# A fused pre-norm linear-attention and FFN kernel: q rotated with channels on partitions, and three data movements handed to DMA

## The reference, cut to what matters

```python
h = layernorm(x)
q, k, v = h @ Wq.T, h @ Wk.T, h @ Wv.T          # each (32, 256, 8, 16)
g = h @ Wg.T
q = q * cos + rotate_half(q) * sin              # the same for k
kv, ksum, vsum = k^T v per head, k.sum(tokens), v.sum(tokens)
num = (q @ kv) * scale + vsum
den = (q . ksum) * scale + 256
o = num / den + conv5(v, lepe_w) + lepe_b       # depthwise conv, 5 taps along the tokens
x = x + (o * g) @ Wo.T
h2 = layernorm(x).astype(bfloat16)
y = (fp8(h2 / s_in) @ fp8(ffn_w / s_k)) * (s_in * s_k)
x = x + (y.astype(bfloat16) + ffn_b)            # written out
```

## Time and profile before

| | |
|---|---|
| Median of 3 runs | 174.56 us (174.33 to 174.72) |
| Profiled execution | 174.49 us, of which the span of the trace is 172.7 us |
| Mean granted PE clock | 0.985 of full speed |
| PE busy / PEld busy | 162.4 us (94%) / 137.7 us (80%) |
| DVE busy | 152.2 us (88%) |
| POOL busy | 137.4 us (80%) |
| ACT busy | 132.5 us (77%) |
| Chain that ended last | PE 85%, POOL 4%, DVE 3%, issue 3%, ACT 2% |

### The profile page before, as it was taken

How to read it: one execution, slowest core, us unless ns; L and a number is a source line. 1 busy time by engine, 2 the same in 40 slices (tenths; PEclk the granted TensorE clock), 3 DMA queues, 4 the chain that set the end, 5 groups by cost and what they waited for, 6 DMA issues and landing times.

```text
span 172.7 us, 3890 instructions
## 1 busy us (share of the span) xinstructions
PE 162.4 (94%) x1140; PEld 137.7 (80%) x1140; DVE 152.2 (88%) x281; ACT 132.5 (77%) x358; POOL 137.4 (80%) x163
## 2 busy tenths in 40 slices
PE   7999999999999999999999999999999999999730
PEld 2578988887879898998889898988998898978510
DVE  2298899989898999999899999989899899899944
ACT  3759757787987878896969888887787786667770
POOL 1468987777897888989898898996889875979871
PEclk9999999999999999999999999999999999999985
DMA  4930002004040404021030404040310220020224
GB/s 133 272 83 0 0 6 61 2 4 121 2 121 6 121 0 123 4 65 56 16 111 0 121 6 121 6 121 0 92 35 0 65 61 4 0 65 2 61 61 121
DMA packets 18966, 9.71 MB, mean 56 GB/s; under 512 B 1536, under 2 KB 18816, under 8 KB 18944
## 3 DMA queue, kind: packets, MB, share of 16 engines
q1 hardware_dynamic: 18368, 9.19, 18.6%
q10 hardware_dynamic: 576, 0.26, 0.6%
HBM read 5.25 MB, written 4.19 MB: 55 GB/s over the span
## 4 chain that ended last, share of the span: by engine, by line
PE 85%; POOL 4%; DVE 3%; issue 3%; ACT 2%; DVEq 0%; POOLq 0%; ACTq 0%
PE bank L1126 15%; PE bank L1210 9%; PE bank L1172 8%; PE p_num L1191 8%; PE bank L1137 8%; PE p_num L1183 8%; PE bank L1145 7%; PE bank L1161 4%; PE bank L1200 4%; PE bank L1116 4%; PE bank L1153 4%; PE bank L1083 3%; PE bank L1253 2%; PE bank L1219 2%; DVE yc L786 1%
## 5 line engine op out<-in xcount | busy, mean ns | idle before, releaser
L597 POOL TENSOR_TENSOR qk<-turned 128x512 f32<-128x512 f32 x32 | 40.3, 1274 | 3.1 <-DVE turned L826 2.9
L826 DVE TENSOR_TENSOR turned<-bank,turn 128x1024 f32<-128x1024 f32 x32 | 38.7, 1216 | 0.9 <-PE bank L1126 0.9
L841 DVE SCALAR_TENSOR_TENSOR acc<-bank,conv_w,acc 128x510 f32<-128x510 f32 (+1 forms) x48 | 34.8, 725 | 0.2
L1126 PE MATMUL bank<-w_qk,hT 128*128 128x256 f32 x128 | 32.8, 381 | 0.2
L370 ACT ACTIVATE h<-x,nmr,rs 128x128 bf16<-128x128 f32 x60 | 24.7, 485 | 3.9 <-POOL nmr L571 3.9
L306 ACT ACTIVATE h<-xs,nmr,rs 128x128 f32<-128x128 f32 x64 | 26.3, 484 | 0.6 <-POOL nmr L560 0.4
L557 POOL TENSOR_TENSOR rs<-ve,minus_half 128x4 f32<-128x4 f32 (+1 forms) x17 | 16.7, 980 | 12.5 <-ACT ve L297 12.5
L1126 PEld LDWEIGHTS bank<-w_qk,hT 128*128 128x128 f32 x128 | 22.6, 190 | 2.9 <-issue 0.3
L568 POOL TENSOR_TENSOR rs<-ve,minus_half 128x4 f32<-128x4 f32 (+1 forms) x17 | 16.6, 977 | 6.7 <-ACT ve L361 6.6
L609 POOL TENSOR_TENSOR acc<-acc,outer 128x508 f32<-128x508 f32 x16 | 20.3, 1271 | 1.0 <-DVE acc L841 1.0
L1137 PEld LDWEIGHTS bank<-w_v,hT 128*128 128x128 f32 x128 | 16.4, 191 | 4.7 <-issue 3.3
(11 more groups left out here) (88 smaller groups left out, 326.6 us busy)
## 6 DMA issues: line engine op xcount, KB each, us to landing
xs<-_attn_hidden_states_dram SPq DMA_DIRECT2D x15, 256.0 KB, 2.8
out_dram<-ob SPq DMA_DIRECT2D x15, 256.0 KB, 2.5
turn<-in_turn_dram SPq DMA_DIRECT2D x1, 512.0 KB, 4.7
xs<-_attn_hidden_states_dram SPq DMA_DIRECT2D x2, 128.0 KB, 2.8
out_dram<-ob SPq DMA_DIRECT2D x2, 128.0 KB, 2.1
mask<-in_mask_dram SPq DMA_DIRECT2D x1, 68.0 KB, 5.0
w_raw<-in_L_attn_Wq_dram ACTq DMA_DIRECT2D x1, 64.0 KB, 2.3
w_raw<-in_L_attn_Wk_dram ACTq DMA_DIRECT2D x1, 64.0 KB, 2.5
```

The lines of the kernel that those rows point to most:

```text
L597: nc.gpsimd.tensor_tensor(qk[:, u % 2, j].rearrange("p q t d -> p t q d"), turned[:, j, :, :, 0:D].rearrange("p a h (q d) -> p (a h) q d", ...
L826: nc.vector.tensor_tensor(turned[:, j], p_qk[j].rearrange("p a h d -> p a (h d)").unsqueeze(2).to_broadcast([P, TPB, 2, 2 * D]), turn[:], ...
L841: nc.vector.scalar_tensor_tensor(out=part, in0=p_vT[:, :, lo + off:hi + off], scalar=conv_w[:, k:k + 1], in1=part, op0=ALU.mult, op1=ALU.a ...
L1126: last = nc.tensor.matmul(p_qk[j][:, a].rearrange("p h d -> p (h d)"), hT[:, u % 3, t * P:(t + 1) * P], w_qk[:].rearrange("p a q d -> p (a ...
```

## The change

The diff has four parts, and with them all five lists of calls are written anew.

1. q is projected alone and with channels on partitions: the weight is the stationary operand and one matmul with 512 columns makes q^T of the unit. DVE multiplies it by cosine and signed sine (`turn_q_unit`). The swap of the channel halves goes across partitions, so two DMAs on SP's queue move 64 partitions each (`swap_q`), and POOL adds (`add_q`). `transpose_q` and `move_qT` are gone. k stays with tokens on partitions and is done for the whole unit at once (`project_k`, `turn_k_unit`, `add_k`).
2. h2 is turned by a transposing DMA on SP's queue (`turn_h2`) for units 0 to 13, and by PE as before for units 14 and 15. ACT quantises from SBUF.
3. The FFN product is one matmul with the weight stationary and 512 columns, so y has channels on partitions. ACT scales it (`move_y`) and in a second instruction adds the bias, which is now one number per partition (`add_bias`). A second transposing DMA turns it back (`turn_yc`), and POOL's `final_sum` reads that. POOL's `add_bias` is gone. The last unit stays as it was.
4. Convolution tap 0 leaves DVE: ACT writes its product to a buffer (`conv_outer(u, 1)`), POOL adds it in a second `sum_outer`.

The core of the diff:

```diff
+            def swap_q(u):
+                s = u % 2
+                sp.wait_ge(q_turned_done, count(u))
+                sp.dma_start(q_swapped[0:P // 2, s], q_turned[P // 2:P, s, 1]).then_inc(q_swapped_in[s], 16)
+                sp.dma_start(q_swapped[P // 2:P, s], q_turned[0:P // 2, s, 1]).then_inc(q_swapped_in[s], 16)
+            def turn_h2(u):
+                s = u % 2
+                sp.wait_ge(h2_done, count(u))
+                if u >= 2:
+                    sp.wait_ge(q8_done, count(u, 2))
+                sp.dma_start(h2T[:, s].rearrange("p (t k) -> p t k", t=TPU), h2[:, s].rearrange("p t d -> p (t d)"),
+                             transpose=True).then_inc(h2T_in[s], 16)
+            def turn_yc(u):
+                s = u % 2
+                sp.wait_ge(ycT_done, count(u))
+                if u >= 2:
+                    sp.wait_ge(ob_done, count(u, 2))
+                sp.dma_start(yc[:, s], ycT[:, s], transpose=True).then_inc(yc_in[s], 16)
...
-                    act.wait_ge(h2T_filled, count(u))
+                    if u < PE_H2:
+                        act.wait_ge(h2T_in[u % 2], h2T_count(u))
+                    else:
+                        act.wait_ge(h2T_filled, 1)
...
+                nc.scalar.activation(ybT[:, u % 2], p_y[:], ACT.Copy, scale=ysc[:, 0:1]).then_inc(yb_done, 1)
+            def add_bias(u):
...
+                nc.scalar.activation(ycT[:, u % 2], ybT[:, u % 2], ACT.Identity,
+                                     bias=fb_act[:, 0:1]).then_inc(ycT_done, 1)
...
+            def add_q(u):
+                s = u % 2
+                pool.wait_ge(q_swapped_in[s], 32 * (u // 2 + 1))
...
+                nc.gpsimd.tensor_tensor(qT[:, s], q_turned[:, s, 0], q_swapped[:, s], ALU.add).then_inc(qT_done, 1)
...
+            def turn_q_unit(u):
...
+                nc.vector.tensor_tensor(
+                    q_turned[:, s].rearrange("p c (j s) -> p c j s", j=BPU),
+                    p_q[:].rearrange("p (j s) -> p j s", j=BPU).unsqueeze(1).to_broadcast([P, 2, BPU, S]),
+                    turn_q[:].unsqueeze(2).to_broadcast([P, 2, BPU, S]), ALU.mult).then_inc(q_turned_done, 1)
...
+            def project_q(u, *freed):
...
+                nc.tensor.matmul(p_q[:], w_qk[:, 0].rearrange("p a d -> p (a d)"), hT[:, u % 3], start=True,
+                                 stop=True).then_inc(q_filled, 1)
...
-                    for t in range(TPU):
-                        last = nc.tensor.matmul(p_y[:, t * P:(t + 1) * P], q[:, t * P:(t + 1) * P], fwq[:],
-                                                start=True, stop=True)
-                    last.then_inc(y_filled, 1)
+                    nc.tensor.matmul(p_y[:], fwq[:], q, start=True, stop=True).then_inc(y_filled, 1)
...
-DVE_TAPS = (1, 3, 0)
-ACT_TAP = 4
+DVE_TAPS = (1, 3)
+ACT_TAPS = (4, 0)
```

More of the change, by code:

```diff
@@ L217, in build @@
         h2T_filled = sem("h2T_filled")
+        h2T_in = [sem(f"h2T_in{n}") for n in range(2)]
         q8_done = sem("q8_done")
@@ new lines, in _ @@
+            load_x(3)
+            swap_q(1)
+            load_x(4)
+            swap_q(2)
+            turn_h2(0)
+            load_x(5)
+            swap_q(3)
+            turn_yc(0)
+            turn_h2(1)
+            load_x(6)
+            swap_q(4)
+            turn_yc(1)
+            turn_h2(2)
+            load_x(7)
+            swap_q(5)
+            turn_h2(3)
+            store(0)
+            store(1)
+            turn_yc(2)
+            load_x(8)
+            swap_q(6)
+            turn_yc(3)
@@ L274, in _ @@
+            store(10)
+            turn_yc(12)
+            turn_yc(13)
+            store(12)
+            store(13)
+            turn_yc(14)
+            store_end(0)
+            store(14)
+            store_end(1)
             sp.wait_ge(ob_free[0], 16 + 16 * (U // 2))
@@ new lines, in _ @@
+            var_eps2(3)
+            move_hT(6)
+            quantise_if_small(2, is_small)
+            norm2(3)
+            move_v(6)
+            var_eps1(7)
+            move_y(2)
+            conv_outer(6, 0)
+            conv_outer(6, 1)
+            add_bias(2)
+            norm1(7)
+            quantise_if_small(3, is_small)
+            conv_middle(6)
+            var_eps2(4)
+            move_hT(7)
+            move_y(3)
+            add_bias(3)
+            for t in range(8, 10):
+                move_v(t - 1)
+                var_eps1(t)
@@ new lines, in _ @@
+            pow2(3)
+            final_sum(1)
+            add_q(5)
+            pow1(7)
+            sum_outer(5, 0)
+            add_k(6)
+            sum_outer(5, 1)
+            final_sum(2)
+            pow2(4)
+            add_q(6)
+            pow1(8)
+            sum_outer(6, 0)
+            add_k(7)
+            final_sum(3)
+            for t in range(9, 12):
+                sum_outer(t - 3, 1)
+                pow2(t - 4)
+                add_q(t - 2)
+                pow1(t)
+                sum_outer(t - 2, 0)
+                final_sum(t - 5)
+                add_k(t - 1)
@@ new lines, in _ @@
+            sum_outer(9, 1)
+            pow2(8)
+            pow1(12)
+            add_q(10)
+            sum_outer(10, 0)
+            final_sum(7)
+            sum_outer(10, 1)
+            add_k(11)
+            pow2(9)
+            add_q(11)
+            pow1(13)
+            sum_outer(11, 0)
+            add_q(12)
+            sum_outer(11, 1)
+            add_k(12)
+            final_sum(8)
+            pow1(14)
+            pow2(10)
+            sum_outer(12, 0)
+            add_k(13)
+            sum_outer(12, 1)
```

992 lines of the change are left out of this document (558 added, 434 removed).

## The result

The changed kernel takes 178.58 us (median of 4 runs, 177.85 to 180.07), the kernel before on the same chip 174.53 us. The ratio is 1.0243, 95% interval 1.0191 to 1.0294: 4.1 us slower. The forecast was 169.5 us, so its sign is wrong; the time lies inside the range of 163.5 to 181. The profiled execution took 180.07 us with a span of 178.3. Every time here is the median of all executions of its kernel; the ratios leave out four executions, each of another kernel, that ran in a slower state of the chip, and without them no median moves by more than 0.07 us.

The account below looks back on a forecast made before the run. PE's list was taken as the bound, DVE about 5% behind. Fourteen units saving 9.45 - 9.0 = 0.45 us give 6.3: 174.49 - 6.3 + 1.3 = 169.5 us; own range 163.5 to 173.9, 8-in-10 range 163.5 to 181.

Parts of the forecast that it names:

- The new waits: Waits on the added DMAs for h2, q's swap and y: hidden in the middle, with 2.8 us taken for a transposing DMA.
- the paragraph on SP's queue: SP's queue goes from two issues a unit to six, about 0.5 us each, so 3.1 of 9 us.
- Both cost nothing in the middle.: q's swap and y's turn back: POOL reads each one period later, so neither costs time in the middle.
- The turn of h2, 2.8 us under 3.35 of cover: ACT's quantisation waits for the turned h2; 3.35 us of other ACT work hides a 2.8 us DMA.
- Rival C: Slow transposing DMA stalls ACT's quantisation by the excess over 3.35 us per unit; 182.7 or 192 us in its cases; chance 0.18.
- PE's list, 8.72 us: PE's work per middle unit falls from 9.45 to 8.72 us, mainly by dropping the transposes of q and h2.
- rival D: The change does not do what it says: given no room, as FFN branches and turns are unconditional for these inputs.
- The 9.0 us that I allowed for waits among level engines: Period of a middle unit, 0.2 us above the largest engine sum; ends 8.8 and 9.3.
- DVE, ACT and POOL: Their work per middle unit after the change: DVE 8.25 us, ACT 8.81, POOL 8.57.
- The end, +1.3 us: Later last norm on ACT and unit 14's y going through a DMA add about 1.3 us; ends 0.5 and 3.5.
- Rival B: Waits in the loop around the PSUM bank shared by h, v and q eat the saving; 174 to 177 us; chance 0.14.
- The signs of being wrong: ACT waiting for h2's DMA every unit, a transposing issue over 1 us on SP, or PE gaps over 0.3 us with others idle.

Follow-up runs that it names:

- no_swap_no_turns: loads_early without the two swap DMAs of q and the two transposing DMAs of h2 and y; output not the reference's; 168.29 us, ratio 0.9643.
- loads_early: The changed kernel with six slots for x instead of four and each load of x from unit 4 on issued one unit earlier; 172.82 us, ratio 0.9909.
- before_loads_early: The kernel before the change, with six slots for x instead of four and each load of x one unit earlier; 174.49 us, ratio 1.0003.
- tap_on_dve: end_ordered with part four of the change undone, so convolution tap 0 is on DVE again; 177.37 us, ratio 1.0142.
- end_ordered: loads_early with POOL's final sum of unit 13 behind unit 15's second-norm powers, and SP's turn of y of unit 14 ahead of unit 13's store; 172.38 us.
- h2_on_pe: loads_early with h2 of units 0 to 10 turned by PE again, in k's PSUM bank; 178.93 us, ratio 1.0276.

## Why the prediction was wrong, by its own steps

The run no_swap_no_turns has neither cost: 178.58 - 5.8 (late loads) - 4.5 (swap and turns) = 168.3 us. That is close to the forecast without its 1.3 us for the end (168.2), in part by luck, as the list below says. What I called hidden was not.

- **The step that failed** is "The new waits", with the paragraph on SP's queue. It counted the six issues rightly (two of 1.2 us, four of 0.4 to 0.6 make 4.5 us and not 3.1), and compared the sum with the period. The queue was never full; it was in order. What mattered is who stands behind whom, and the load of x, which the change does not touch, was not looked at. Its cost was put at nothing without a word. DVE's 4.8 us between the last reader of a slot and the next statistics was the cover that made it free. The new list has 3.1 there, by 1.13 us because a rotation moved ahead of the residual and by 0.66 because a tap left; the prediction priced DVE's sum and did not ask what in the list had been cover. Price: 5.8 us (loads_early against after; before_loads_early as control).
- **"Both cost nothing in the middle."** Swap 1.7 us and turn of y 2.0, by leaving each out. Each has slack in its own pair of instructions, but stands behind other entries, or makes others late.
- **The turn of h2, 2.8 us under 3.35 of cover.** The landing was right: 2.4 us at least, 2.5 in the median. But it reached 4.1, and 4.3 in loads_early, and ACT waited 5.5 us (3.5). Price 3.1 us. Rival C had this mechanism with its place, but as a steady excess; it came only in some units. The Trainium skill, page VectorE: DVE Perf Modes, section The three transpose paths, has 1309 ns for one 128x128 piece by DMA; the estimate of 5.2 us made from it, by taking four in a row, does not hold for one DMA of 128x512, at 2.5, and a single piece was not measured here. The Trainium skill, page Advanced Engine Details and Errata, section X-Bar Transpose, says that such DMAs are as fast as plain ones; the trace agrees for the landing (2.5 against 2.7 for the plain swaps) and not for the issue (1.2 us against 0.5 to 0.6).
- **PE's list, 8.72 us.** PE was full at 9.12 (no_swap_no_turns), and at 8.75 without the branches, so the pieces were priced right in sum. What the list lacked is that the branches hold the FFN piece and its neighbours when the quantisation ends late, 0.37 us in a steady unit; rival D even called the branches unconditional, which they are not. The row I took for the FFN (82.35 to 82.70, 0.35 us) was a slow one too: in five other units of the kernel before, the same four pieces took 0.23 to 0.25. So the saving in a steady unit was 9.45 - 9.13 = 0.32 us and not 0.73. The 9.0 us that I allowed for waits among level engines took up most of that, since this is such a wait.
- **The sum without DMAs.** That 168.3 meets 168.2 is in part luck. The span is 6.2 us shorter than before (172.7 and 166.5), and it is made up otherwise than in the forecast, which had 14 times 0.45: 0.6 us because the transposes of t1 of unit 1 come earlier (32.48 and 31.85), which the prediction counted as zero; 5.4 in the 13 periods that follow (120.6 and 115.2 us); 1.4 in the last unit's period (8.32 and 6.89); and 1.2 lost behind it.
- **DVE, ACT and POOL** at 8.25, 8.81 and 8.57: measured 8.36, 8.67 and 8.38 in that same clean period. Right, within 0.2 us. That the tap should leave DVE was right as well (tap_on_dve).
- **The end, +1.3 us.** From the last transpose of t1 to the end of the span it was 11.3 us before (161.41 to 172.7) and 13.5 after (164.79 to 178.3), so +2.2; inside its ends of 0.5 to 3.5. Without any of the new DMAs it is 12.5 (153.96 to 166.5), so +1.2 is there without them, as much as I priced for the moves ahead of the last norm on ACT, and about 1.0 comes with them. Of that the order on POOL and SP is a small part: end_ordered won at most about 0.4 us.
- **Rival B** (waits in a loop) is nearest to what happened in kind, and its 174 to 177 us is nearest in size, but the loop is another: slot of x, SP's queue, statistics, first norm, projections, residual.
- **The signs of being wrong.** Two of three came: one transposing issue occupied SP's queue for 1.2 us, and PE had 1.1 us of gaps in a period (10.85 less 9.77) while the others idled too. The third did not: ACT waited for the turned h2 in 6 units, not in every one.
- **What would have shown it**: the kernel before has DVE's residual, the issue of the load and the statistics in its timeline. Three rows give 4.8 us of cover, and the order of DVE's new list gives what is left.

What stays open: whether a second queue for swaps or turns would win the remaining 4.5 us (not tried), how much of h2_on_pe's loss a better place would avoid, and how much of the late loads is place in the queue and how much slower landing.

## What to carry to other kernels

When a change shortens or reorders an engine's list, look at what the work that left or moved was covering: find for each buffer its last reader and the next user of the load that refills it, and compare the distance with issue plus landing. When it adds DMAs to an in-order queue, write the queue out with what each entry waits for; its sum over a period says little. More buffers and an earlier load cost one constant and a shift of the loads in SP's list here, and turned 2.4% slower into 1% faster.

## What the runs showed of the hardware beyond this

A transposing DMA of 128x512 bf16 inside SBUF held SP's queue for 1.19 to 1.21 us (median), against 0.5 to 0.6 for a plain one of 128 KB, and landed 2.5 us after its issue (median; 2.4 to 4.6). Two branches around one short matmul of PE cost 0.37 us a period (9.12 against 8.75) where what it waited for ended 0.3 us before it, nothing where that had ended 0.8 us before, and 2.0 us in all.
